# A decoder layer on one core: weight folding reordered by first use of its loads, feed-forward rows two quarters ahead, last outputs in four banks

## The reference

```
x = x + latent_attention(layernorm(x))          # 16 heads, keys and values from a latent of 64
x = x + cross_attention(layernorm(x), ctx, mask)  # 1500 context rows for each sequence
x = x + feed_forward(layernorm(x))
feed_forward(x) = fp8(gelu(fp8(x) @ fp8(Wg0)) * (fp8(x) @ fp8(Wg1))) @ fp8(Wlinear)   # 256 -> 1024 -> 256
```

## Time and profile before

| | us |
|---|---|
| median of 3 runs | 1647.14 (1645.62 to 1651.4) |
| profiled execution, own time | 1644.11 |
| its span, first to last instruction | 1642.3 |
| fold_weights | 0 to 52.2 |
| feed_forward | 1539.2 to 1642.3 |
| mean granted TensorE clock over the span | 0.976 |

### The profile page before, as it was taken

One profiled execution on the slowest core, in us unless ns is written; L12 is line 12 of the kernel. 1 busy time (PEld: TensorE's weight loads), 2 busy tenths in 40 slices (PEclk: granted clock), 3 DMA queues, 4 the chain that ended last, 5 costly groups with the idle time before them and its releaser, 6 DMA issues. The chain is left out here.

```text
span 1642.3 us, 44152 instructions
## 1 busy us (share of the span) xinstructions
PE 1529.4 (93%) x18130; PEld 1304.8 (79%) x18130; DVE 1361.7 (83%) x2391; ACT 1106.2 (67%) x2099; POOL 626.7 (38%) x656
## 2 busy tenths in 40 slices
PE   5999999998869999999999999999999999999367
PEld 5788888887548888888888888888888888888246
DVE  3798888888448898998988989989889899888576
ACT  2666666665447777777777777777777777777475
POOL 0465656565143343333333333333333333332201
PEclk9999999999989999999999999999999999999679
DMA  7000000000031111111111112111111111110001
GB/s 229 7 1 1 1 1 1 2 1 2 1 121 52 47 44 59 58 39 59 51 58 47 51 58 59 39 59 52 55 49 51 52 51 40 52 52 2 1 12 35
DMA packets 44505, 67.92 MB, mean 41 GB/s; under 512 B 9557, under 2 KB 42770, under 8 KB 44178
## 3 DMA queue, kind: packets, MB, share of 16 engines
q1 hardware_dynamic: 44306, 65.11, 13.4%
HBM read 63.26 MB, written 1.84 MB: 40 GB/s over the span
## 5 line engine op out<-in xcount | busy, mean ns | idle before, releaser
L1243 POOL TENSOR_TENSOR xa_CW<-xa_CTX,xa_CH 128x500 fp32r<-128x500 f32 x187 | 242.6, 1297 | 505.5 <-DVE xl_ACC L1482 421.1
L1438 ACT ACTIVATE xl_PB<-banks,xl_BIB,xl_SCB 125x896 f32<-125x896 f32 x384 | 400.8, 1095 | 38.0 <-PE banks L1290 38.0
L1482 DVE TENSOR_TENSOR xl_ACC<-xl_ACC,xl_PB 125x896 f32<-125x896 f32 x320 | 373.2, 1166 | 11.0
L1473 DVE TENSOR_SCALAR xl_PB<-xl_PB 125x896 f32<-125x896 f32 x384 | 318.0, 831 | 47.1 <-ACT xl_PB L1438 45.7
L1256 PE MATMUL banks<-xa_WVhigh,xa_CH 128*125 128x256 f32 x768 | 235.1, 306 | 0.0
L1420 ACT ACTIVATE xl_V<-banks 125x512 f32<-125x512 f32 x192 | 114.9, 599 | 177.2 <-PE banks L1256 177.1
L1256 PE MATMUL banks<-xa_WVhigh,xa_CW 128*125 128x256 f32 x768 | 216.6, 282 | 0.0
L1256 PE MATMUL banks<-xa_WVlow,xa_CH 128*125 128x256 f32 x768 | 216.4, 282 | 0.0
L1489 DVE SCALAR_TENSOR_TENSOR xl_KXlow<-banks,xa_bk,xl_KXhigh 128x500 fp32r<-128x500 f32 x192 | 137.1, 714 | 68.2 <-ACT xl_KXhigh L1411 68.2
L1306 PE MATMUL banks<-xl_PB,xl_V 125*32 125x112 f32 x6144 | 167.5, 261 | 1.9 <-DVE xl_PB L1473 1.9
L1256 PEld LDWEIGHTS banks<-xa_WVhigh,xa_CH 128*125 128x125 f32 x768 | 142.9, 186 | 27.1 <-issue 16.3
(11 more groups left out here) (240 smaller groups left out, 3726.5 us busy)
## 6 DMA issues: line engine op xcount, KB each, us to landing
xa_CTX<-in_ctxT SPq DMA_DIRECT2D x96, 500.0 KB, 3.5
fw_QUT<-in_W_quT SPq DMA_DIRECT2D x1, 2048.0 KB, 13.0
fw_WO<-in_W_o SPq DMA_DIRECT2D x1, 2048.0 KB, 18.7
xl_RAW<-in_w_gating SPq DMA_DIRECT2D x8, 256.0 KB, 3.8
X<-in_x SPq DMA_DIRECT2D x1, 1792.0 KB, 9.4
out<-ff_R SPq DMA_DIRECT2D x16, 112.0 KB, 1.9
xl_RAW<-in_w_linear SPq DMA_DIRECT2D x4, 256.0 KB, 4.4
QThigh<-in_ku SPq DMA_DIRECT2D x1, 520.0 KB, 13.0
```

The source lines that it names most:

```text
L1243: nc.gpsimd.tensor_tensor(context_piece(CW, i), context_piece(CTX, i), context_piece(CH, i), ALU.subtract).then_inc(ctx_low, 1)
L1438: nc.scalar.activation(PB[t % PR][:, :, :], banks[0:TK, 2 * i:2 * i + KT, 0:QW], ACT.Exp, scale=SCB[j][:, t:t + 1], bias=BIB[j][:, t:t + 1 ...
L1473: nc.vector.tensor_scalar(pt, pt, E_HI, E_LO, ALU.min, ALU.max).then_inc(clipped, 1)
L1482: nc.vector.tensor_tensor(ACC[j][:, :, :], prev[:, :, :], PB[t % PR][:, :, :], ALU.add).then_inc(summed, 1)
```

## The change

In `fold_weights` the loads are issued in another order (W_qu, ku, b_qu and BQ2 first, then x; the loads of `fold_in` last), BQ2 gets a semaphore `bq_in` of its own, and three engines do their work in another order: PE the one-column products first, DVE the copies to BQ ahead of the norm, ACT the square root after the four groups' copies and the transposed blocks' copies after the high parts. WL2 is no longer made by POOL at the start of `feed_forward` but by ACT in pairs 14 and 15 of `cross_loop`. In `feed_forward` DVE makes the rows of two quarters at the start and then of quarter it+2; `turn` follows m = 2 and not 5, outputs follow n = 12 to 15, 20 to 23, 28 to 31 (OUT_LAG 4); four outputs remain after the loop, the last two in banks 4 and 5, and seven of their eight blocks m are issued for all four before the eighth. Outputs wait block by block (`t_ready`, `rest_ready` of m).

```diff
-                sp.dma_start(X[:, :, :], d["x"].rearrange("(g t) h -> t g h", t=T)).then_inc(x_in, 16)
-                sp.dma_start(ident[:, :], d["ident"]).then_inc(ident_in, 16)
                 sp.dma_start(QUT[:, :, :], d["W_quT"]).then_inc(qk_in, 16)
                 sp.dma_start(KUA[:, :, :], d["ku"]).then_inc(qk_in, 16)
                 sp.dma_start(BQU[:, :], d["b_qu"]).then_inc(qk_in, 16)
-                sp.dma_start(BVU[:, :], d["b_vu"]).then_inc(fold_in, 16)
-                sp.dma_start(VUT[:, :, :], d["W_vuT"]).then_inc(fold_in, 16)
-                sp.dma_start(WO[:, :, :], d["W_o"].rearrange("(h p) n -> p h n", p=P)).then_inc(fold_in, 16)
-                sp.dma_start(BO[:, :], d["b_o"]).then_inc(fold_in, 16)
+                sp.dma_start(BQ2[0:RD, :], d["b_qr"][0:RD, :]).then_inc(bq_in, 16)
+                sp.dma_start(BQ2[RD:P, :], d["b_qr"][RD:P, :]).then_inc(bq_in, 16)
+                sp.dma_start(X[:, :, :], d["x"].rearrange("(g t) h -> t g h", t=T)).then_inc(x_in, 16)
+                sp.dma_start(ident[:, :], d["ident"]).then_inc(ident_in, 16)
...
+                sp.dma_start(BVU[:, :], d["b_vu"]).then_inc(fold_in, 16)
+                sp.dma_start(VUT[:, :, :], d["W_vuT"]).then_inc(fold_in, 16)
+                sp.dma_start(WO[:, :, :], d["W_o"].rearrange("(h p) n -> p h n", p=P)).then_inc(fold_in, 16)
+                sp.dma_start(BO[:, :], d["b_o"]).then_inc(fold_in, 16)
...
-                norm_vector(nc, dve, n1, X)
-                for g in range(PAIRS):
-                    normalize(nc, n1, XN[:, g, :], X, g).then_inc(xn_ready, 1)
                 dve.wait_ge(small_done, 1)
-                dve.wait_ge(attn_in, 16 * ATTN_LOADS)
+                dve.wait_ge(bq_in, 16 * 2)
                 for b in range(2):
                     r, l = slice(b * RD, (b + 1) * RD), slice((1 - b) * RD, (2 - b) * RD)
                     nc.vector.tensor_copy(BQ[r, b::2], BQ2[r, :])
                     mm = nc.vector.tensor_copy(BQ[l, b::2], bank[6][l, 0:NH // 2])
                 mm.then_inc(small_read, 1)
+                norm_vector(nc, dve, n1, X)
+                for g in range(PAIRS):
+                    normalize(nc, n1, XN[:, g, :], X, g).then_inc(xn_ready, 1)
...
-                norm_scalar(nc, act, n1)
...
-                transpose_copies(nc, act, XT, bank, bank_read, turned)
+                norm_scalar(nc, act, n1)
...
+                transpose_copies(nc, act, XT, bank, bank_read, turned)
...
+                for h in range(NH):
+                    lo = (1 - h % 2) * RD
+                    mm = nc.tensor.matmul(bank[6][lo:lo + KVC, h // 2:h // 2 + 1], KUA[:, h, 0:KVC], BQU[:, h:h + 1],
+                                          start=True, stop=True)
+                mm.then_inc(small_done, 1)
...
+                        if s == 8 and g >= PAIRS - 2:
+                            act.wait_ge(w_ready, ALL_PIECES)
+                            at = slice((g - PAIRS + 2) * FT * H // 2, (g - PAIRS + 3) * FT * H // 2)
+                            nc.scalar.activation(WL2[:, at], WL8[:, at], ACT.Copy, scale=2.0).then_inc(w_twice, 1)
...
-        ROWS_AT, TURN_AT, OUT_LAG = {1: 0, 2: 1, 3: 2, 4: 3}, 5, 6
+        ROWS_AT, TURN_AT, OUT_LAG = {2: 0, 3: 1, 4: 2, 5: 3}, 2, 4
...
+        def output_bank(g):
+            return bank[6 + g % 2 if g < PAIRS - 2 else 4 + g % 2][0:T, 0:H]
...
-                def output(g):
+                def output(g, blocks=range(FT)):
-                    pe.wait_ge(t_ready, it * FT + FT)
-                    pe.wait_ge(rest_ready, it * FT + FT)
-                    if p == 0:
-                        pe.wait_ge(bank_read, KT * min(SUP, it + 3))
-                    if g >= 2:
-                        pe.wait_ge(y_ready, g - 1)
-                    for m in range(FT):
+                    if blocks[0] == 0:
+                        if p == 0:
+                            pe.wait_ge(bank_read, KT * min(SUP, it + 3))
+                        if g >= PAIRS - 2:
+                            pe.wait_ge(gate_ready, FF_UNITS - 2)
+                            pe.wait_ge(up_ready, FF_UNITS - 2)
+                        elif g >= 2:
+                            pe.wait_ge(y_ready, g - 1)
+                    for m in blocks:
+                        pe.wait_ge(t_ready, it * FT + m + 1)
+                        pe.wait_ge(rest_ready, it * FT + m + 1)
                         for part, w in ((T8, WL8), (D8, WL2)):
-                            mm = nc.tensor.matmul(bank[6 + g % 2][0:T, 0:H], part[it % len(part)][:, m, p * T:(p + 1) * T], w[:, m * H:(m + 1) * H],
-                                                  start=(m == 0 and part is T8), stop=(m == FT - 1 and part is D8))
-                    mm.then_inc(y_done, 1)
+                            mm = nc.tensor.matmul(output_bank(g), part[it % len(part)][:, m, p * T:(p + 1) * T], w[:, m * H:(m + 1) * H],
+                                                  start=(m == 0 and part is T8), stop=(m == FT - 1 and part is D8), skip_group_check=True)
+                    if blocks[-1] == FT - 1:
+                        mm.then_inc(y_done, 1)
...
-                pe.wait_ge(twice_ready, 1)
...
-                for g in range(outputs_before(FF_UNITS), PAIRS):
-                    output(g)
+                for g in range(PAIRS - PPS, PAIRS):
+                    output(g, range(FT - 1))
+                for g in range(PAIRS - PPS, PAIRS):
+                    output(g, range(FT - 1, FT))
...
-                nc.gpsimd.tensor_scalar(WL2[:, :], WL8[:, :], 2.0, None, ALU.mult).then_inc(twice_ready, 1)
...
-                for g in range(PPS):
-                    rows(g)
-                widen(0)
+                for s in range(2):
+                    for p in range(PPS):
+                        rows(s * PPS + p)
+                    widen(s)
...
-                    if it + 1 < SUP and m in ROWS_AT:
-                        rows((it + 1) * PPS + ROWS_AT[m])
+                    if it + 2 < SUP and m in ROWS_AT:
+                        rows((it + 2) * PPS + ROWS_AT[m])
                         if ROWS_AT[m] == PPS - 1:
-                            widen(it + 1)
+                            widen(it + 2)
```

More of the change, by code:

```diff
@@ L86, in build @@
         WL8 = ctx.enter_context(nc.sbuf_tensor("WL8", [P, FT * H], BF16))
-        mem = (bank, X, (MV2, MV3, WG8, WL8), ident, banks)
+        WL2 = ctx.enter_context(nc.sbuf_tensor("WL2", [P, FT * H], BF16))
+        mem = (bank, X, (MV2, MV3, WG8, WL8, WL2), ident, banks)
         cross_attention(nc, d, mem, QT, WQ, bq)
@@ L198, in fold_weights @@
     XT, WD, bD, Aq, AqS, U, BQ, CC, WKR, WKS, BKR, BQS, BKS, WVO, OB, COS, SIN, MASK = la
-    ATTN_LOADS = 21
+    ATTN_LOADS = 19
     with ExitStack() as stack:
@@ L219, in fold_weights @@
         n1 = norm_buffers(sb, sem, "n1")
-        x_in, ident_in, qk_in, fold_in, attn_in = sem("x_in"), sem("ident_in"), sem("qk_in"), sem("fold_in"), sem("attn_in")
+        x_in, ident_in, qk_in, fold_in, attn_in = sem("x_in"), sem("ident_in"), sem("qk_in"), sem("fold_in"), sem("attn_in"); bq_in = sem("bq_in")
         zeroed, ones_ready, prod_ready, bvb_ready = sem("zeroed"), sem("ones_ready"), sem("prod_ready"), sem("bvb_ready")
@@ L255, in _ @@
                 sp.dma_start(bD[:, :], d["b_d"]).then_inc(attn_in, 16)
-                sp.dma_start(BQ2[0:RD, :], d["b_qr"][0:RD, :]).then_inc(attn_in, 16)
-                sp.dma_start(BQ2[RD:P, :], d["b_qr"][RD:P, :]).then_inc(attn_in, 16)
                 sp.dma_start(BQS[:, :], d["b_qr_swapped"]).then_inc(attn_in, 16)
@@ L348, in _ @@
                         mm.then_inc(qa_done, 1)
-                for h in range(NH):
-                    lo = (1 - h % 2) * RD
-                    mm = nc.tensor.matmul(bank[6][lo:lo + KVC, h // 2:h // 2 + 1], KUA[:, h, 0:KVC], BQU[:, h:h + 1],
-                                          start=True, stop=True)
-                mm.then_inc(small_done, 1)
                 pe.wait_ge(ones_ready, 1)
@@ L1109, in cross_loop @@
         CN = sb("CN", [P, KT, T])
-        _MV2, MV3, _WG8, _WL8 = ffm
+        _MV2, MV3, _WG8, _WL8, WL2 = ffm
         DL = sb("DL", [T, H])
@@ L1131, in cross_loop @@
         raw_in = [sem(f"raw_in{i}") for i in range(2)]
+        w_twice = sem("w_twice")
         w_half, w_top, w_clamped, w_rest, w_ready = (sem(s) for s in ("w_half", "w_top", "w_clamped", "w_rest", "w_ready"))
@@ L1617, in feed_forward @@
         sb, sem = tools(nc, stack, "ff")
-        _MV2, MV3, WG8, WL8 = ffm
+        _MV2, MV3, WG8, WL8, WL2 = ffm
         IDB = sb("IDB", [P, P], BF16)
@@ L1633, in feed_forward @@
         D8 = [sb(f"D8{i}", [P, FT, N], BF16) for i in range(2)]
-        WL2 = sb("WL2", [P, FT * H], BF16)
-        twice_ready = sem("twice_ready")
         Y = [sb(f"Y{i}", [T, H], BF16) for i in range(2)]
@@ L1774, in keep_output @@
                         dve.wait_ge(r_ready, g - 1)
-                    nc.vector.tensor_copy(Y[g % 2][:, :], bank[6 + g % 2][0:T, 0:H]).then_inc(y_ready, 1)
```

(1 more changed line is left out.)

## The result

The changed kernel takes **1636.54 us** (median of 5 runs, 1635.13 to 1639.53) against 1647.14 for the kernel before: a ratio of 0.9936 (95% interval 0.992 to 0.9951), 10.6 us less. The prediction was 1627.4 with a range of 1620 to 1636.5. The direction is right; the gain is 10.6 us where 19.7 were forecast, and the time lies just outside the range.

The account below looks back on a forecast made before the run. feed_forward was read as bound by waits, paced by ACT, and fold_weights as one chain; -5.8 + 0.3 - 3.35 - 8.6 - 2.3 = -19.7 us took the median from 1647.14 to 1627.4, range 1620 to 1636.5.

Parts of the forecast that it names:

- Fold: fold_weights: reordered loads and work end the stage at 46.0 against 51.9, -5.8 us, bounds -7 to -2.
- 9.1: fold_weights: the qk_in loads, now first in the queue, land at 9.1 us (8.5 to 12).
- I put W_o at 29 to 34.5: fold_weights: W_o, now last in the queue, lands at 29 to 34.5 us; up to 1.5 us could be lost.
- BVB takes 1.7 more: fold_weights: POOL's copy to BVB, after W_o's landing and ahead of L365, takes 1.7 us.
- the start of L365 to the end took 11.3: fold_weights: from the start of L365 to the stage's end takes 11.3 us, as before.
- W_o late: Rival, fold_weights: W_vu and W_o land at 41.1, stage ends at 54.1, +2.2 us, total 1635.4; chance 0.14.
- The table load: fold_weights, ACT before the square root: load costs 1.28 us without a 1.38 drain; with the drain the term would be -4.4.
- Start of feed_forward: Start of feed_forward: with POOL idle, DVE's four rows take 1.36 us in place of 4.71, -3.35 us.
- Stalls: feed_forward, first to last gate copy: ACT's stalls fall from 15.6 to 7 us, -8.6.
- Tail: Last gate copy to the end of the last R: 13.3 us (13.0 to 14.8) in place of 15.6, -2.3.
- PE's lead: Rival, feed_forward outputs: PE's lead covers them, stalls of 3 not 7, qk_in at its lower bound, 1621.7; chance 0.13.
- third rival: feed_forward: the turn's wait is only replaced; four outputs in a row wait for bank and Y, 1635; chance 0.08.

Follow-up runs that it names:

- mid_both: `wo_mid` with DVE copying the output to Y at the start of its step and the turn behind m = 1: 1625.01 us, ratio 0.9864.
- lows_after: Changed kernel, but DVE waits for BVB before its three low-part subtractions: 1633.96 us, ratio 0.9928.
- bvb_early: Changed kernel, but POOL's copy to BVB waits for the load of b_vu alone, and PE for the other fold_in loads: 1630.68 us, ratio 0.9909.
- wl2_pool: Changed kernel, but WL2 is made by POOL at the start of feed_forward again, not by ACT: 1640.14 us, ratio 0.9958.
- ff_only: Changed kernel with the fold_weights of the kernel before: 1632.35 us, ratio 0.9927.
- tail_two_banks: Changed kernel with the last four outputs issued as wholes in banks 6 and 7: 1636.98 us, ratio 0.994.
- wo_mid: Changed kernel with fold_in's loads right behind x and ident, and ACT's XT copies ahead of its high parts: 1628.72 us, ratio 0.9896.

## Why the prediction was wrong

**What bounds the kernel**, the reading of feed_forward as a stage of waits, held: 15.6 us of stalls became 8.0, the XB waits went to zero, and the step of ACT stayed at 1.78. When the last two waits were moved (`mid_both`) first to last gate copy came within 1.6 us of the 58.8 that was worked out for it.

**Fold, the step that failed.** The prediction had the chain at 46.0; it ended at 56.1. By its steps:
- "9.1" for qk_in was 11.36 us, in part since the loads flowed at 348 GB/s from 2 to 9 us and not at 407. The transposes were done at 37.45 in place of 34.7, +2.75, of which 2.3 are this landing. It lies within the bounds given (8.5 to 12), at the far end.
- "I put W_o at 29 to 34.5": 36.06 us. In this execution that alone would have cost next to nothing, since 36.06 + 1.68 = 37.7 is 0.3 behind the transposes. Where the group landed at 38.27 (`lows_after`) it cost 2.03 us of idle and 1.8 in L366.
- "BVB takes 1.7 more": this is the step that failed. It took 6.30, since it now lies beside three DVE subtractions, +4.7 (`lows_after`, `bvb_early`). I had moved the instruction in time and counted its length as if it ran alone, without asking what runs on DVE at its new place, although the same effect, with the engines exchanged, was the reason of the term for the start of feed_forward. The two readings belong together: whoever takes -3.35 for a contention that goes away has to look for contentions that come.
- "the start of L365 to the end took 11.3": 13.67, +2.4, of which 2.35 are L365 at the low clock behind 4.96 us of idle.
- 2.75 + 4.96 (PE's wait for the copy, from 37.45 to 42.41) + 2.4 = 10.1, the whole miss of this term.

The bounds of the term, -7 to -2, had no room for this. The rival that came closest, W_o late at 1635.4, had the place right and the mechanism mostly wrong: its 54.1 came from a landing at 41.1, and the latest seen was 38.33. That its time is near the measured 1636.54 is luck.

**The table load.** What the row of before showed held again: the copy ahead ends at 28.10, the load stands at 28.11, the square root at 29.41, 0.02 us behind the load's end. The drain of 1.38 us that the prediction weighed is seen on neither side.

**WL2 on ACT** cost nothing: the stretch up to feed_forward is 0.25 shorter. **Start of feed_forward** -3.4 against -3.35, and `wl2_pool` gives it back by the mechanism named. **The second quarter's rows** took 1.38 + 0.69 us on DVE and were hidden, as argued. **Stalls** -7.5 against -8.6, a matter of size. The three turns had held 7.4 us of ACT's waits and not 8.0, as its first product behind each waited 0.43 and not 0.6; and what is left is 8.0 and not 7, of which 2.78 is one wait at the last gate copy, behind PE's wait for Y of 2.20. That PE wait is longer than a step of 1.78, which the prediction had named as a sign of being wrong; the other two for Y, 0.41 and 0.74, are not. **Tail** -2.05 against -2.3, with some luck: at the clock of `ff_only` and `lows_after` the same tail is 15.24 us, 0.4 below that of before, and the forecast had the low clock at 14.8 at most. That the separate banks and the split blocks make the gain is not shown (`tail_two_banks`).

**The rivals.** The clock did not stay low; feed_forward's rose from 0.79 to 0.90. PE's lead did not cover the outputs: stalls of 3 would have been needed, 8.0 were left. The turn's wait was replaced only in small part: the 2.12 for XB and up to 2.20 for Y on PE are those of the third rival, but ACT's waits behind them are 7.3 in all in three groups, as the main case had it.

## What to carry to other kernels

Before an instruction of POOL or DVE is moved, lay the other's timeline over its new place: here the one that came second stood still for as long as the other's run lasted (6.30 us for 1.68 on POOL, 3.75 for 0.41 on DVE), and twice it was the one on the critical path. Let an instruction wait for the load that it reads and not for the group in which that load is counted; the copy to BVB needed 8 KB and waited for 2.7 MB. Waits that share one lead (here for XB and for Y) have to be looked at together: moving XB's alone only moved the time to Y's (+0.7 us), moving Y's alone won 4.6, and both won 6.5.

## What was not expected of the hardware

- By its ends POOL's copy of 128x1792 stood still over the rest of three successive DVE instructions and not of one (start 36.06 or 37.27, end 42.36 or 42.39, 1.68 when alone). DVE's first cast behind it then waited in its turn: 1.85 us for two where the next two took 0.48.
- Where the same copy came first, DVE paid and not POOL: in `bvb_early` it started at 30.39, 0.50 us ahead of DVE's sixteen XN rows, and kept its 1.68; the rows took 6.18 us and not 5.26.
- An idle time of 4.96 us on PE cost another 2.35 in the clock; one of 2.03 cost 1.7 to 1.8 (L366 at 8.85 against 7.07 to 7.13), nearly as much. There the granted clock was still 1.00 from 38 to 40, in the idle time, 0.76 from 40 to 42 and 0.50 from 42 to 44, when PE was busy again. The 3.6 us of idle ahead of the transposes cost nothing that shows: in `wo_mid` the clock stayed at 1.00 and L365 took 7.07.
- The same loads landed up to 2.3 us apart in different executions of the same order (W_o's group at 36.06, 37.27, 38.27 and 38.33).
